# Twelve tiles of edge codes made in three column parts from chunk 3 of pass 1, two more places for expanded weights, and two shares moved ahead of the last quad

## What is computed

```
# layer 0: two gated graph steps with the same adj, relu after each
def _ggc(x, adj, W, wih, whh, bih, bhh):
    m = adj @ (x @ W)
    gi = m @ wih.T + bih
    gh = x @ whh.T + bhh
    r = sigmoid(i_r + h_r);  z = sigmoid(i_z + h_z)
    n = tanh(i_n + r * h_n)
    return (1.0 - z) * n + z * x
x = _layernorm(x + relu(_ggc(relu(_ggc(x, ...)), ...)))
# layer 1: each row keeps its last 100 neighbours, weighted by rank
support = x @ weight
mask = (adj != 0)
rank = cumsum(mask, axis=1);  deg = rank[:, -1:]
k = minimum(deg, 100.0);      pos = rank - (deg - k)
w = mask * where(pos > 0, 0.5 ** (k - pos), 0.0)
x = _layernorm(x + (w @ support + bias))
```

## Time and profile before

| engine | busy us | share of the span |
|---|---|---|
| TensorE matmul (PE) | 337.7 | 93% |
| VectorE (DVE) | 297.4 | 82% |
| ScalarE (ACT) | 184.3 | 51% |
| GpSimd (POOL) | 23.9 | 7% |

### The profile page before, as it was taken

One profiled execution on the slowest core, in us unless ns is written; L12 is line 12 of the kernel. 1 busy time (PEld: TensorE's weight loads), 2 busy tenths in 40 slices (PEclk: granted clock), 3 DMA queues, 4 the chain that ended last, 5 costly groups with the idle time before them and its releaser, 6 DMA issues.

```text
span 363.6 us, 6494 instructions
## 1 busy us (share of the span) xinstructions
PE 337.7 (93%) x2416; PEld 156.3 (43%) x2424; DVE 297.4 (82%) x479; ACT 184.3 (51%) x237; POOL 23.9 (7%) x32
## 2 busy tenths in 40 slices
PE   1998999999999999999999999999899999998972
PEld 1343233333333333333333324453344554887962
DVE  0689889897876976979996577899999999798983
ACT  0202404131041310575295377857796869776992
POOL 2000000000000000000000010202020202102242
PEclk9999999999999999999999999999999999999998
DMA  7999999999999999998889999898969994000011
GB/s 248 413 408 409 408 411 406 410 408 370 409 379 339 399 336 319 326 348 311 287 286 390 402 411 385 298 351 314 387 233 386 359 376 158 16 4 2 2 60 58
DMA packets 32719, 111.08 MB, mean 306 GB/s; under 512 B 3633, under 2 KB 6193, under 8 KB 32689
## 3 DMA queue, kind: packets, MB, share of 16 engines
q1 hardware_dynamic: 31824, 109.20, 79.4%
q10 hardware_dynamic: 864, 1.48, 1.2%
HBM read 109.62 MB, written 1.05 MB: 304 GB/s over the span
## 4 chain that ended last, share of the span: by engine, by line
PE 70%; DMA 9%; DVE 9%; ACT 6%; issue 4%; POOL 1%; POOLq 0%; ACTq 0%; DVEq 0%
PE m_acc L439 37%; PE out L439 15%; DMA stream<-in_adj_t 8%; PE out L544 4%; DVE run L931 3%; PE rz_ps L517 2%; PE rz_ps L503 2%; PE n_ps L544 2%; DVE codes L936 2%; DMA w<-in_w 2%; PE rz_ps L496 2%; PE n_ps L496 2%; PE rz_ps L544 1%; ACT s_in L717 1%; PE m_acc L544 1%
## 5 line engine op out<-in xcount | busy, mean ns | idle before, releaser
L439 PE MATMUL m_acc<-stream,s_in 128*64 128x512 f32 x512 | 125.9, 607 | 3.7 <-issue 2.3
L887 DVE TENSOR_SCALAR codes<-stream 128x1024 uint8<-128x1024 f32 x117 | 76.4, 685 | 4.2 <-DMA stream<-in_adj_t 4.0
L439 PE MATMUL out<-stream,s_mid 128*64 128x512 f32 x272 | 69.1, 595 | 0.8 <-DMA stream<-in_adj_t 0.6
L439 PEld LDWEIGHTS m_acc<-stream,s_in 128*64 128x64 f32 x512 | 33.9, 137 | 66.3 <-issue 53.3
L439 PE MATMUL m_acc<-stream,s_mid 128*64 128x512 f32 x240 | 53.9, 597 | 0.0
L827 POOL TENSOR_TENSOR rstd<-var,mhalf 128x4 f32<-128x4 f32 x16 | 22.0, 1378 | 336.0 <-DVE var L1042 336.0
L936 DVE SCALAR_TENSOR_TENSOR codes<-codes,run 128x1024 uint32<-128x1024 uint32 (+2 forms) x42 | 40.8, 970 | 1.4
L931 DVE TENSOR_TENSOR run<-run,codes 128x2048 uint16<-128x2048 uint16 (+2 forms) x41 | 39.3, 960 | 1.6
L627 ACT ACTIVATE m_high<-m_acc 64x512 f32<-64x512 f32 x13 | 7.7, 595 | 58.8 <-PE m_acc L439 45.7
L717 ACT ACTIVATE wexp<-codes,code_bias 128x2048 uint16<-128x2048 uint8 x18 | 35.7, 1993 | 0.6 <-DVE codes L936 0.5
L439 PEld LDWEIGHTS out<-stream,s_mid 128*64 128x64 f32 x272 | 19.1, 137 | 39.2 <-issue 38.8
(11 more groups left out here) (150 smaller groups left out, 406.0 us busy)
## 6 DMA issues: line engine op xcount, KB each, us to landing
stream<-in_adj_t SPq DMA_DIRECT2D x204, 512.0 KB, 6.1
x_res<-in_x_pairs SPq DMA_DIRECT2D x8, 128.0 KB, 6.6
out_nodes<-stream SPq DMA_DIRECT2D x8, 128.0 KB, 1.9
hx<-in_x_pairs ACTq DMA_DIRECT2D x1, 512.0 KB, 7.4
const<-in_consts ACTq DMA_DIRECT2D x1, 358.0 KB, 6.6
hx<-in_x_pairs ACTq DMA_DIRECT2D x2, 128.0 KB, 6.2
hx<-in_x_pairs ACTq DMA_DIRECT2D x1, 256.0 KB, 8.9
bias_b<-in_bias SPq DMA_DIRECT2D x1, 128.0 KB, 4.9
```

The costliest lines, as they stand in the source:

```text
L439: last = nc.tensor.matmul(to[D * u:D * (u + 1), :], state[:, t * D:(t + 1) * D], stream[:, n % SLOTS, u * CW:(u + 1) * CW], start=start[u] ...
L887: nc.vector.tensor_scalar(edges(p // 2, b, 2 * (p % 2), 2), stream[:, n % SLOTS, :], 0.0, None, ALU.not_equal).then_inc(mask_made, 1)
```

## The change

Three things are changed. First, `chain` in pass 1 works in three parts of the columns instead of two: chunks 0 to 2, 3 to 5 and 6 to 7. Twelve tiles are done by parts instead of ten: twelve for the first part from chunk 3 on (three tiles in chunk 3, four each in chunks 4 and 5, one in chunk 6), twelve for the second part in chunks 6 and 7, and twelve for the third at the pass's end and in pass 2 as before. Second, there are two more places, `h` (in `hx`, the state of chunks 4 to 7) and a second use of `k`; with them every later block gets another place, and 21 blocks instead of 19 are expanded by VectorE. Third, shares (5, 5) and (6, 5) come ahead of the quad (7, 0) to (7, 3).

```diff
-EARLY = NCH - 2
-CHAIN_EARLY = {6: {10: 1, 11: 1, 12: 1, 13: 1, 14: 1}, 7: {2: 1, 4: 1, 6: 1, 8: 1, 10: 1}}
+PARTS = (slice(0, 3), slice(3, 6), slice(6, NCH))
+GUARD_IN = {3: 0, 6: 1}
+CHAIN_EARLY = ({3: (11, 13, 15), 4: (4, 7, 10, 13), 5: (4, 7, 10, 14), 6: (4,)},
+               {6: (10, 11, 12, 13, 14, 14), 7: (2, 4, 6, 8, 10, 12)})
+N_EARLY = sum(len(steps) for steps in CHAIN_EARLY[0].values())
...
-     (7, 0), (7, 1), (7, 2), (7, 3), (7, 4), (5, 5), (6, 5), (7, 5)] + \
+     (5, 5), (6, 5), (7, 0), (7, 1), (7, 2), (7, 3), (7, 4), (7, 5)] + \
...
-PLACES = ["w0", "w1"] + [f"s{i}" for i in range(SLOTS)] + ["m"] + [f"d{i}" for i in range(1, 10)]
+PLACES = ["h", "k", "w0", "w1"] + [f"s{i}" for i in range(SLOTS)] + ["m"] + [f"d{i}" for i in range(1, 10)]
...
-               6: (1, 2, 2), 7: (1, 1, 1), 8: (1, 1, 4)}
-DVE_EXPANDS = {1: (0, 0, 0), 2: (0, 0, 0), 3: (0, 0, 0), 4: (0, 0, 1), 5: (0, 0, 1), 6: (0, 0, 0),
-               7: (0, 0, 2), 8: (3, 1, 4)}
-ACT_END = (1, 1, 1, 1, 1, 1, 1, 0)
-DVE_END = (1, 1, 1, 1, 1, 1, 1, 0)
+               6: (1, 2, 2), 7: (1, 1, 1), 8: (1, 1, 3)}
+DVE_EXPANDS = {1: (0, 0, 0), 2: (0, 0, 0), 3: (0, 0, 0), 4: (0, 0, 1), 5: (0, 0, 1), 6: (0, 0, 1),
+               7: (1, 0, 2), 8: (2, 1, 4)}
+ACT_END = (2, 1, 1, 1, 1, 0, 0, 0)
+DVE_END = (2, 2, 1, 1, 1, 1, 0, 0)
...
-CHAIN = [chain_tiles(*x) for x in ((0, 4), (4, 9), (9, 14), (14, 19), (19, 23), (23, 27), (27, 31),
+CHAIN = [chain_tiles(*x) for x in ((0, 5), (5, 10), (10, 15), (15, 19), (19, 23), (23, 27), (27, 31),
                                    (31, 32), (32, 32))]
-CHAIN_CUT = [(1, 2), (2, 4)] + [(1, 2)] * (NCH - 1)
+CHAIN_CUT = [(1, 2), (2, 4), (2, 3)] + [(1, 2)] * 4 + [(0, 1)] * 2
...
+            if place == "h":
+                return hx[:, N // 4:N // 2].bitcast(BF16)
...
+                if PLACE[j, i] == "h":
+                    act.wait_ge(h_made, NCH + 4)
...
-            def guard(late):
+            def guard(part):
-                dve.wait_ge(start_made, NCH if late else EARLY)
-                at = run[0][:, EARLY * CW:] if late else run[0][:, 0:EARLY * CW]
+                chunks = PARTS[part]
+                dve.wait_ge(start_made, chunks.stop)
+                at = run[0][:, chunks.start * CW:chunks.stop * CW].bitcast(U16)
...
-                to = slice(0, NCH) if KT * j + KT - 1 - k >= N_EARLY else \
-                    slice(EARLY, NCH) if late else slice(0, EARLY)
+                to = PARTS[part] if KT * j + KT - 1 - k < N_EARLY else slice(0, NCH)
```

More of the change, by code:

```diff
@@ L128 @@
 PLACE.update({block: (PLACES + AGAIN + AGAIN)[n] for n, block in enumerate(REST)})
-BY_DVE = [AHEAD[4], AHEAD[6]] + [REST[n] for n in (4, 6, 8, 10, 12, 14, 15, 17, 18, 20, 22, 24, 26, 28, 30, 32, 34)]
+BY_DVE = [AHEAD[4], AHEAD[6]] + [REST[n] for n in (2, 3, 5, 7, 9, 11, 12, 14, 16, 18, 19, 21, 22, 24, 26, 28, 30, 32,
+                                         34)]
 BY_ACT = [(0, 0), (0, 1), (0, 2), (0, 3), (1, 0), (1, 1), (1, 2), AHEAD[0]] + \
@@ L186, in chain_tiles, with codes_count @@
     return [(n // KT, KT - 1 - n % KT) for n in range(first, last)]
-def codes_count(j, k, late=True):
-    n = KT * j + KT - 1 - k
-    return n + 1 + (N_EARLY if late else 0)
-CHAIN = [chain_tiles(*x) for x in ((0, 4), (4, 9), (9, 14), (14, 19), (19, 23), (23, 27), (27, 31),
+def codes_count(j, k, part=2):
+    return KT * j + KT - k + part * N_EARLY
+CHAIN = [chain_tiles(*x) for x in ((0, 5), (5, 10), (10, 15), (15, 19), (19, 23), (23, 27), (27, 31),
                                    (31, 32), (32, 32))]
-CHAIN_CUT = [(1, 2), (2, 4)] + [(1, 2)] * (NCH - 1)
+CHAIN_CUT = [(1, 2), (2, 4), (2, 3)] + [(1, 2)] * 4 + [(0, 1)] * 2
 def build(nc, adj_t, x_pairs, w1, consts, bias, out):
@@ L910, in fold_sums, with chain @@
                         .then_inc(sum_made, 1)
-            def guard(late):
-                dve.wait_ge(start_made, NCH if late else EARLY)
-                at = run[0][:, EARLY * CW:] if late else run[0][:, 0:EARLY * CW]
-                nc.vector.tensor_scalar(at.bitcast(U16), at.bitcast(U16), float(GUARD * 257),
-                                        None, ALU.add).then_inc(guarded, 1)
-            def chain(j, k, late=True):
-                c, n, i = NCH - 1 - j, tile_step(j, k), codes_count(j, k, late)
-                to = slice(0, NCH) if KT * j + KT - 1 - k >= N_EARLY else \
-                    slice(EARLY, NCH) if late else slice(0, EARLY)
+            def guard(part):
+                chunks = PARTS[part]
+                dve.wait_ge(start_made, chunks.stop)
+                at = run[0][:, chunks.start * CW:chunks.stop * CW].bitcast(U16)
+                nc.vector.tensor_scalar(at, at, float(GUARD * 257), None, ALU.add)\
+                    .then_inc(guarded, 1)
+            def chain(j, k, part=2):
+                c, n, i = NCH - 1 - j, tile_step(j, k), codes_count(j, k, part)
+                to = PARTS[part] if KT * j + KT - 1 - k < N_EARLY else slice(0, NCH)
                 if n == 0:
-                    dve.wait_ge(guarded, 2 if late else 1)
+                    dve.wait_ge(guarded, part + 1)
                 if i > 1:
@@ L1015, in _ @@
                             keep_add(b - 1)
-                    if b == EARLY and q == GUARD_AT:
-                        guard(False)
-                    if b in CHAIN_EARLY and q in CHAIN_EARLY[b]:
-                        for _ in range(CHAIN_EARLY[b][q]):
-                            chain(*chain_tiles(early, early + 1)[0], False)
-                            early += 1
+                    if b in GUARD_IN and q == GUARD_AT:
+                        guard(GUARD_IN[b])
+                    for part, steps in enumerate(CHAIN_EARLY):
+                        for _ in range(steps.get(b, ()).count(q)):
+                            chain(*chain_tiles(early[part], early[part] + 1)[0], part)
+                            early[part] += 1
                     if b == 1 and q == 9:
@@ L1089, in _ @@
             new_h(NCH - 1)
-            guard(True)
+            guard(2)
             for j, k in CHAIN[0]:
```

5 lines of the change are left out of this document (3 added, 2 removed).

## The result

The changed kernel took 359.94 us (median of 5, 358.84 to 360.22), the kernel before 365.21 us (median of 5, 364.94 to 365.83). The ratio is 0.985, with a 95% interval of 0.983 to 0.987. The profiled execution took 359.25 us with a span of 357.1 us (before 363.6); the granted clock is 0.998. The forecast was 358.3 us. The spans of the five executions lie at 357.0 and 357.1, and at 358.1 to 358.2 us; the profiled one is of the first kind, and the experiments on the turn come back to this difference of 1.1 us.

The account below looks back on a forecast made before the run. TensorE, busy 93% of the span, was taken as the bound. The terms 0 - 1.2 - 2.2 + 1.7 - 5.2 = -6.9 us took 365.44 to 358.5 us profiled; forecast 358.3 us, range 356.0 to 362.0 us.

Parts of the forecast that it names:

- The turn: From pass 1 to pass 2: chunk 7's loads land some 1.5 us earlier, saving 1.2 us; bounds 0 and 1.5.
- Pass 1 costs nothing: Chunks 3 to 5: VectorE's added tiles cost 0; without cover, up to 0.3 us a chunk, about 1 us.
- margin of 2.7: Chunk 3: combine 3.0 us later against 2.7 us before TensorE's gates; 0.3 us late at most.
- the straight line through the earlier trace: VectorE tiles in pass 1: 768 columns cost 1.26 us, on the line between 0.99 and 2.06 us.
- The waits for `h_c`: TensorE at node(10) and node(11): both waits go with fewer tiles ahead of n_input, -2.2 us; ends -0.4 and -2.6.
- rival 4: More gain: node(15) is not late and short TensorE waits on ScalarE go too; 356.3 us, chance 0.09.
- node(15), +1.7 us: At t = 7: two more VectorE expansions and the moved codes instruction make node(15) 1.7 us later; ends 0 and 2.8.
- The rule of the Trainium skill on the shared port pair: VectorE with two SBUF inputs and GpSimd exclude each other; at t = 7 the instruction order costs 0.9 us.
- The tail, -5.2 us: From node(15) to the last share's end: 34.0 us become 28.8; ends -2.5 and -5.2.
- Part 4: Places and order of shares: nine shares instead of seven ahead of the last quad, so its wait goes; tail -5.2 us.

Follow-up runs that it names:

- e10: e5 plus 28 small unused products on TensorE at the start, shifting all later TensorE instructions by 112 places; 357.88 us, ratio 0.979.
- e5: Changed kernel with the 128 KB load of x_res for pass 2's first step issued in chunk 7 of pass 1, not at the turn; 358.85 us, ratio 0.981.
- e2: Changed kernel with the tiles as before the change; new places, share order and expansion tables kept; 362.3 us, ratio 0.991 to the kernel before.
- e3: Changed kernel's tiles alone; places, share order, expansions and the last codes instruction as before the change; 363.06 us, ratio 0.992 to the kernel before.
- e4: Changed kernel with the last tile's codes instruction back ahead of the sum at t = 7; 358.65 us, ratio 0.981 to the kernel before.
- e8: Changed kernel with VectorE's expansion ahead of n_input at t = 7 moved behind that step's combine; 358.12 us, ratio 0.980 to the kernel before.
- e9: Changed kernel with shares (5, 5) and (6, 5) behind the last quad again; 359.17 us, ratio 0.983 to the kernel before.

## Why the prediction was right, and where it was not

**Right in the sign, and near in the size.** For the profiled execution it gave 358.5 us where 359.25 was measured. The turn is 1.4 us of the miss (node(7) to node(8) was to lose 1.2 us and grew by 0.2, from 12.5 to 12.7); the stretch from node(8) to node(13) gives 0.7 of it back, the start 0.2, and what lies outside the span grew by 0.3 us (from 365.44 - 363.6 to 359.25 - 357.1). So the total is nearer than its parts, and that is luck: a term that was not there was in part made up for by others that came out larger.

**Pass 1 costs nothing: right, with two sizes off.** `combine` on VectorE and chunk 4's gates on TensorE, for the earlier trace rows:

```profile
96.60 0.68 DVE L962 TENSOR_TENSOR mx<-m_acc,m_high 64x512 f32<-64x512 f32 x1
```

```profile
97.94 0.60 PE L501 MATMUL rz_ps<-mx,const 128*64 128x256 f32 x4
```

`combine` is 1.8 us later and not 3.0, against a margin of 2.7. In chunk 3 a tile costs less than the 1.26 us of the straight line through the earlier trace rows:

```profile
102.43 0.55 DVE L938 TENSOR_TENSOR run<-run,codes 128x768 uint16<-128x768 uint16 x1
103.02 0.56 DVE L943 SCALAR_TENSOR_TENSOR codes<-codes,run 128x384 uint32<-128x384 uint32 x1
103.49 0.69 DVE L894 TENSOR_SCALAR codes<-stream 128x1024 uint8<-128x1024 f32 x1
```

From its start to the next instruction are 1.06 us. The line had been drawn through tiles that stand behind one another; here a mask or the combine follows, which does not depend on the tile. Where two tiles do stand behind one another, in chunk 6, their starts lie the forecast 1.26 us apart:

```profile
155.90 0.56 DVE L938 TENSOR_TENSOR run<-run,codes 128x768 uint16<-128x768 uint16 x1
...
157.16 0.56 DVE L938 TENSOR_TENSOR run<-run,codes 128x768 uint16<-128x768 uint16 x1
```

**The turn, -1.2 us: wrong, it was +0.2.** The step that failed is that the loads of chunk 7 "land some 1.5 us earlier, and that counts at the turn". The first half was right. SyncE's waits from 170 to 197 us, for the earlier trace rows:

```profile
SPq L398 <- PE out L444: 10.4, 12, 1.3
SPq L397 <- DVE codes L894: 7.4, 6, 2.1
```

The waits for masks went from 15.5 to 7.4 us, and pair 126 landed 3.3 us earlier (186.8 against 190.1 us). But the ring has seven slots, so load 132 goes out when TensorE has used pair 125, at 192.0 us after the change and 192.3 before; what had been waits for VectorE became waits for TensorE. From there a pair lands each 1.28 us and is used in 0.86, so the lead is used up by pair 139, and the landings set node(8). The lead that the earlier masks gave is lost in the ring. What was to be had at the turn lay in the landings themselves: cleared of a 128 KB load and of one instruction packet, they gave e10 11.3 us from node(7) to node(8), where the changed kernel has 12.7. With only the load taken away (e5) it was 12.5.

**The waits for `h_c`, -2.2 us: right, a little small.** For the earlier trace rows, ScalarE's first sigmoid at t = 3 and `n_input` behind it:

```profile
237.70 0.47 ACT L664 ACTIVATE rz<-rz_ps,b_rz 128x256 f32<-128x256 f32 x1 [1.30 <-PE n_ps L508]
...
238.21 0.48 DVE L971 SCALAR_TENSOR_TENSOR t_n<-rz_ps,const,rz 128x256 f32<-128x256 f32 x1 [0.15 <-ACT rz L664]
```

VectorE now waits for ScalarE there. From node(8) to node(11) are 2.6 us less. The 0.4 us over the forecast are a short wait for ScalarE's weights behind node(10) (a gap of 0.21 us before, and as much again inside the modelled matmuls), and the same behind node(11) gives another 0.4 us up to node(12); rival 4 had them as "short waits of TensorE on ScalarE". e2 and e3 show that the tiles alone bring this.

**node(15), +1.7 us: right, 1.75, with the parts shared out otherwise.** node(14) came 0.5 us later against node(13) and not 0.8, and 1.3 us were added behind it and not 0.9. For the earlier trace rows, VectorE and GpSimd at t = 7:

```profile
307.24 0.47 DVE L971 SCALAR_TENSOR_TENSOR t_n<-rz_ps,const,rz 128x256 f32<-128x256 f32 x1
...
312.69 0.42 DVE L1045 TENSOR_REDUCE stat<-sq 128x4 f32<-128x256 f32 x1 [0.87 <-ACT sq L705]
313.14 0.17 DVE L1049 TENSOR_SCALAR var<-stat 128x4 f32<-128x4 f32 x1
313.22 1.23 DVE L943 SCALAR_TENSOR_TENSOR codes<-codes,run 128x1024 uint32<-128x1024 uint32 x1
```

```profile
313.39 1.92 POOL L834 TENSOR_TENSOR rstd<-var,mhalf 128x4 f32<-128x4 f32 x1 [14.09 <-DVE var L1049]
```

Taken out one at a time, the tile's instruction beside `rstd` is worth 0.7 us (e4; 0.9 in the sum) and the expansion ahead of `n_input` 1.0 us (e8; 0.8 in the sum). The rule of the Trainium skill on the shared port pair that the prediction weighed holds in e4: without a VectorE instruction beside it, `rstd` takes 1.01 us.

**The tail, -5.2 us: right in the size, partly wrong in the cause.** The 28.8 us were met. Part 4 had the quad's wait go because nine shares instead of seven lie ahead of it; e9 shows that seven do. The two places and the two expansions less on ScalarE did it together.

**Why the median moved less than the profile.** The profiled executions differ by 6.2 us, the medians of the first measurement by 5.3. Three of its five executions had a span 1.1 us longer. e4's profile shows one way to lose that much: the slips at `x_res` and at the packet were 1.3 and 1.5 us there, where the changed kernel's profile has 0.4 and 1.0. That the three were of this kind is argued and not shown, since none of them was profiled. A fallen clock as in e2 would be the other candidate; the execution at 359.94 us has a mean clock of 0.997, above e2's 0.994, which speaks against it there.

## What to carry to other kernels

A wait taken from a queue of loads pays only up to the next thing that hands out its slots; so follow the freed loads to the first landing that TensorE waits for, and count slots and landing interval on the way, before a gain is booked there. Where the price of one delay varies from kernel to kernel (here 0 to 1.5 us for one packet), the gain from taking away a smaller one beside it is lost in that; only the kernels with neither showed it clearly. When a stretch grows although nothing in it waits, read the granted clock there before you look for a late producer. And put filler work of an in-order engine where it waits anyway (here behind the combine), not ahead of the instruction that others wait for.
